# A two-engine sum in a fused attention stage: both adds of the neighbour sum on GpSimd

## The reference, cut to what matters

```python
attn = jnp.einsum('bhnd,bhmd->bhnm', q, k) * D ** (-0.5)
kernel = jnp.ones((KS, KS), dtype=attn.dtype).at[KS // 2, KS // 2].set(0.0)
neigh = lax.conv_general_dilated(attn.reshape(B * H, 1, N, N), kernel, window_strides=(1, 1), padding='SAME', ...)
attn = attn - BETA * neigh.reshape(B, H, N, N)
attn = jax.nn.softmax(attn - jnp.max(attn, axis=-1, keepdims=True), axis=-1)
```

## Time and profile before

| | before |
|---|---|
| median of three runs | 2139.98 us |
| the profiled execution | 2124.2 us |
| span of its profile | 2122.0 us |
| PE busy in the span | 1845.8 us (87%) |
| DVE busy | 1494.5 us (70%) |
| ACT busy | 1267.0 us (60%) |
| POOL busy | 1136.7 us (54%) |
| mean granted TensorE clock | 0.94 of full |

### The profile page before, as it was taken

How to read it: one execution, slowest core, us unless ns; L and a number is a source line. 1 busy time by engine, 2 the same in 40 slices (tenths; PEclk the granted TensorE clock), 3 DMA queues, 4 the chain that set the end, 5 groups by cost and what they waited for, 6 DMA issues and landing times. The chain is left out here.

```text
span 2122.0 us, 54414 instructions
## 1 busy us (share of the span) xinstructions
PE 1845.8 (87%) x17949; PEld 1383.3 (65%) x17949; DVE 1494.5 (70%) x4652; ACT 1267.0 (60%) x2469; POOL 1136.7 (54%) x1069
## 2 busy tenths in 40 slices
PE   4868888888888888888897479999999999999991
PEld 3656666666666666666664357777777777777760
DVE  4769999999999999999996345656565555554430
ACT  4657878878788888878887224444444444433330
POOL 4334555556464555556452346666676767654442
PEclk8879999999999999999998559999999999999995
DMA  4475665656565565656554248888888888899887
GB/s 153 145 207 173 185 187 176 187 182 202 159 198 179 176 186 168 189 189 202 159 155 124 84 139 203 189 215 191 210 193 211 191 211 188 201 200 184 183 145 197
DMA packets 362727, 382.72 MB, mean 180 GB/s; under 512 B 144532, under 2 KB 326096, under 8 KB 358288
## 3 DMA queue, kind: packets, MB, share of 16 engines
q1 hardware_dynamic: 320912, 338.66, 54.8%
q0 software_dynamic: 41664, 42.12, 12.0%
HBM read 232.83 MB, written 135.46 MB: 174 GB/s over the span
## 5 line engine op out<-in xcount | busy, mean ns | idle before, releaser
L1793 DVE SCALAR_TENSOR_TENSOR ml<-mid_bank,mh 128x512 bf16<-128x512 f32 x336 | 232.1, 691 | 330.6 <-ACT mh L1881 329.5
L1881 ACT ACTIVATE mh<-mid_bank 128x512 bf16<-128x512 f32 x336 | 200.6, 597 | 410.6 <-PE mid_bank L1572 410.6
L1060 ACT ACTIVATE probs<-t_bank 98x392 f32<-98x392 f32 x768 | 341.8, 502 | 141.5 <-PE t_bank L651 139.7
L859 DVE TENSOR_REDUCE row_max<-s_bank 98x2 f32<-98x392 f32 x768 | 395.2, 557 | 34.3 <-PE s_bank L635 32.7
L1947 POOL DMA_INDIRECT sums<-y_out,tail x168 | 265.1, 1578 | 158.5 <-DVE y_out L1823 111.0
L1589 PE MATMUL y_bank<-wst,ml 128*128 128x192 bf16 x1344 | 330.1, 246 | 0.0
L1586 PE MATMUL y_bank<-wst,mh 128*128 128x192 bf16 x1344 | 330.1, 246 | 0.0
L1588 PE MATMUL y_bank<-wst,mh 128*128 128x192 bf16 x1344 | 329.9, 245 | 0.0
L635 PE MATMUL s_bank<-k_stack,q_stack 96*98 96x196 f16 x1536 | 232.9, 258 | 82.8 <-DVE row_max L859 68.0
L651 PE MATMUL t_bank<-q_stack,k_stack 104*98 104x196 f16 x1536 | 220.1, 256 | 37.3 <-ACT probs L1060 34.9
L1228 POOL TENSOR_TENSOR x_lo<-x_buf,x_hi 128x588 f16<-128x588 f32 x128 | 166.4, 1312 | 157.8 <-DVE tilde L947 66.9
(11 more groups left out here) (236 smaller groups left out, 4518.2 us busy)
## 6 DMA issues: line engine op xcount, KB each, us to landing
wst<-packed SPq DMA_DIRECT2D x56, 1584.0 KB, 8.3
x_buf<-in_x_t SPq DMA_DIRECT2D x32, 1176.0 KB, 7.8
q_stack<-stack_parts SPq DMA_DIRECT2D x288, 98.0 KB, 2.5
k_stack<-stack_parts SPq DMA_DIRECT2D x288, 98.0 KB, 2.6
stack_parts<-qk_hi SPq DMA_DIRECT2D x32, 588.0 KB, 2.9
stack_parts<-qk_lo SPq DMA_DIRECT2D x32, 588.0 KB, 3.1
sums<-h_buf SPq DMA_DIRECT2D x32, 294.0 KB
h_in<-sums SPq DMA_DIRECT2D x32, 294.0 KB
```

Of the source, the lines that this page charges most:

```text
L859: nc.vector.reduce_max(row_max[st.odd][:, :, hh:hh + 1], s_bank[hh % 2][0:HALF, :, 0:TOKENS], AX.X).then_inc(max_ready, 1)
L1060: nc.scalar.activation(probs[st.odd][:, hh], t_bank[hh % 2][0:HALF, :, 0:TOKENS], ACT.Exp).then_inc(probs_ready, 1)
L1793: nc.vector.scalar_tensor_tensor(ml[n % MID][:], mid_bank[n % MID_PS][:], 0.0, mh[n % MID][:], ALU.max, ALU.subtract).then_inc(ml_ready, 1)
L1881: nc.scalar.activation(mh[n % MID][:], mid_bank[n % MID_PS][:], ACT.Relu).then_inc(mh_ready, 1)
```

## The change

The pool engine makes both sums, one behind the other. VectorE's `add_tilde` is gone with both its calls (the one that fills the pipeline and the one in iteration k = 0), and so is the pool engine's wait for `tilde_ready`.

```diff
-            def add_tilde(pr):
-                if pr.there:
-                    dve.wait_ge(beside_ready, pr.u + 1)
-                    wait(dve, tilde_hi_ready, pr.u)
-                    nc.vector.tensor_tensor(tilde[:], beside[:], padded[:, :, 1:TOKENS + 1], ALU.add
-                                            ).then_inc(tilde_ready, 1)
...
-                add_tilde(first)
                 take_v(first, 0)
...
-                    if k == 0:
-                        add_tilde(Pair(body, kk, 1))
-                    elif k == 1:
+                    if k == 1:
                         take_low_tilde(Pair(body, kk, 1))
...
                     nc.gpsimd.tensor_tensor(beside[:], padded[:, :, 0:TOKENS], padded[:, :, 2:PW], ALU.add
                                             ).then_inc(beside_ready, 1)
+                    pool.wait_ge(beside_ready, pr.u + 1)
+                    wait(pool, tilde_hi_ready, pr.u)
+                    wait(pool, tilde_lo_ready, pr.u)
+                    nc.gpsimd.tensor_tensor(tilde[:], beside[:], padded[:, :, 1:TOKENS + 1], ALU.add
+                                            ).then_inc(tilde_ready, 1)
...
                 if k == 0:
                     add_beside(Pair(body, kk, 1))
-                    if Pair(body, kk, 1).there:
-                        pool.wait_ge(tilde_ready, Pair(body, kk, 1).u + 1)
                     split_patches(Pair(body, kk, 2), (3,))
```

## The result

The changed kernel took 2170.38 us (median of four runs, 2168.82 to 2172.86), the kernel before 2138.44 us beside it: ratio 1.0162, interval [1.0141, 1.0183]. It is slower by 32 us.

A forecast was written before the change was run, and what follows sets the result against it. TensorE was taken to bound k = 0, then VectorE's chain from the maxima of k = 1. Delays of 2 + 15 = 17 us plus 11 for the clock gave +28 us, 2168 us; 8-in-10 range 2134 to 2205.

The forecast's parts named there:

- kind A: 17 of the 32 pairs, with TensorE the limit in k = 0: 0.1 us lost a pair, 2 us.
- the clock: TensorE falling to half clock as it idles longer: in every second kind B pair, 6.5 x 1.74 = 11 us.
- its own signs: In k = 0, L867 near 2 us and L870 near 1.3 in kind B; 0.17 and about 2.1 in kind A.
- kind B: 13 pairs behind the iteration packing expert weights: maxima of k = 1 late by 1.42 us, 1.14 net, 15 us.
- Who is first in kind A: New pool sum against VectorE's L867 after `beside`: practically a tie, L867 taken as first, 0.1 us a pair.
- the first rival: The pool sum goes first in kind A too: maxima 1.2 us late net, +61 us, 2201 us; chance 0.22.
- The room in VectorE's chain: After late maxima of k = 1, only the reciprocal's idle time, 0.28 or 0.29 us, gives any delay back.
- The rival of no change: Splits slip in before the pool sum, or later idle time absorbs the delay: 2140 us, within 6; chance 0.18.
- The faster rival: VectorE's work is the limit, so a lighter k = 0 pays: up to 44 us gone, 2096 us; chance 0.12.

The follow-up runs named there:

- e4: Kernel before, with VectorE's tilde add cut to 2 of 196 columns and all waits kept: 2121.0 us, ratio 1.0003.
- e1: Changed kernel, with the pool engine's tilde sum of k = 0 waiting until VectorE has made both maxima splits: 2122.0 us, ratio 1.0003 to the kernel before.
- e2: Changed kernel, with the pool engine's `x_lo` of k = 0 waiting for both splits: 2122.0 us, ratio 1.0011 to the kernel before.
- e3: Kernel before, with only the pool engine's wait for `tilde_ready` ahead of `x_lo` taken out: 2121.4 us, ratio 1.0007.
- e7: The changed kernel again, nothing altered, in another set of runs: 2156.6 us against 2120.3 for the kernel before, ratio 1.0170.
- e5: Kernel before, with the pool engine's residual sum of k = 1 moved behind VectorE's tilde low part: 2083.4 us, ratio 0.9821.
- e6: Changed kernel, with the residual sum of k = 1 moved behind VectorE's tilde low part: 2131.1 us, ratio 0.9973 to the kernel before.

## Why the prediction was right, and where it was not

The prediction said 2168 us against 2170.4 measured, and slower with 0.70. Its mechanism is the one found: the add on VectorE was hidden (e4), the pool engine's sums hold the two splits (the timelines above), and putting them behind the splits takes the whole loss away (e1). But that the number came so close is luck: two errors of its sum cancel, 17 us too little for kind A and some 10 too much for the clock. Of its own signs those of kind B came (L867 2.13 us, L870 1.24), those of kind A did not (2.42 and 1.24 instead of 0.17 and 2.1).

**Who is first in kind A: wrong.** The prediction took the pool engine to need 0.17 to 0.25 us from the end of `beside` to its next sum, from two nearest rows and "two more waits", and so let L867 go first, at a cost of 0.1 us. The gap is 0.08 us. Only the tie of less than 0.1 us was seen; it fell the other way, and the first rival's mechanism is what happened, in every pair of kind A in the stage's steady part. They cost 1.1 us each instead of 0.1, 17 x 1.0 = 17 us more than the sum had. That rival's time, 2201 us, did not come, mostly because of its 26 us for the clock.

**Kind B: right in size, by parts that are not.** 1.14 us were predicted. Pairs with the same `beside` compared, the maxima of k = 2 come at 12.98 us instead of 11.92 (`beside` 2.22 us), and at 13.21 instead of 12.14 (2.44 us): 1.06 and 1.07 late. The distance from a kind B pair to the next pair, without a fall, is 34.40 instead of 33.34, 1.06 too. The tilde sum takes 2.48 us and not 2.15 (inside the bounds 2.14 to 2.79) but starts 0.09 to 0.17 sooner, so that the maxima of k = 1 are 1.52 late where 1.42 was predicted. The chain gives back 0.45 of it and not 0.28.

**The room in VectorE's chain: wrong.** "The rest of VectorE's chain has no other idle time to give back" overlooked that the wait of kind "issue" before the plain low part shortens when VectorE arrives late (0.23 for 0.33 us), and that the reciprocal follows the maxima 0.37 us closer where 0.29 was taken. The edit itself gave another 0.13 us before the tilde low part. My expectations for e2 and e3 carried the same error, and those runs showed it.

**TensorE's clock: more falls than predicted, at a much smaller price.** I put 11 us on 6.5 more falls at 1.74 us. There are ten more, 16 in the steady part instead of 6, and the granted clock is 0.97 for 0.99. But the 16 together cost 915.99 - 13 x 69.56 = 12 us and the 6 cost 11, so the clock adds 1 us, or 3 by e7's profile. The two runs without a fall agree: between e5 and e6 the change costs 27.1 us over 26 pairs, and the change itself costs 29.3. In the kernel before a fall costs 1.6 to 2.1 us over two pairs. In the changed kernel one at the same place costs 1.1 (`beside` at 613.89, 649.89 and 684.53: 70.64 us instead of 69.56). Two single ones on the way from kind B to kind A cost next to nothing, 34.42 and 34.43 us for 34.40. That the cheap ones fall where TensorE then waits for VectorE anyway is likely, but it was argued and not tried.

With what was measured the sum is 30 x 1.1 = 33 us and 1 to 3 for the clock, against 32 measured (30 to 39 by the interval) and 36 in e7. The prediction had 17 and 11. **The rival of no change** was right that a delay can be made up within the pair and wrong on its size: one hold is made up but for 0.05 to 0.12 us (e2, e3), two are not. **The faster rival** is ruled out by e4 and e1.

## What to carry to other kernels

Before moving an elementwise operation from VectorE to the pool engine, list VectorE's small instructions with operands in SBUF alone that run in that time: each can be held for a whole pool instruction, and the cost is the part of the delay beyond the room on the chain to the next waiting engine, here 0.5 to 0.6 us. Look for such a hold among the waits a kernel already has: an instruction whose duration in one place is six times its duration elsewhere is the sign, and moving the pool engine's instruction by one wait (e5) was worth 1.8%, two thirds of it from the hold and one third from falls of the clock that were gone too. A busy share of 92%, holds included, did not make VectorE's work the limit: taking 1.2 us of it away in each pair changed nothing.

## What the runs showed of the hardware that I had not expected

- The pool engine starts a sum 0.08 us after the end of the one whose semaphore it waits for, with two further satisfied waits between; 0.16 and 0.17 us were the nearest rows before.
- Two pool sums of one shape, 128 x 1176 float32 from two SBUF inputs, took 2.15 and 2.48 us. The second reads a contiguous tile and the rows of `padded` from column 1 on; the first reads the rows of `padded` twice, from column 0 and from column 2. Why it is the faster one is open.
- Where `x_lo` follows the tilde sum, the second small instruction never got in between the two pool instructions: L867 ends at 618.64, L870 starts 0.02 us later and is held all the same.
- The kernel before took 2120 to 2138 us from one set of runs to the next, more than half of the effect measured, while its ratio to the changed kernel held: 1.0162 and 1.0170.
- With the residual sum moved, the clock of TensorE stayed at 1.00 over the stretch in both e5 and e6, though in e6 the splits are held as in the changed kernel, whose clock is 0.97. What prevents the falls is open.
